# A chain of attentions on one core: two inputs turned by DMA and VectorE, the mask and its row minimum in one operation, the context exponential moved into the copy out of the bank

## The reference

```python
# block 0: two attentions of 16 heads of 16, then a feed-forward
Q = einsum(x, Wq) * m;  K, V = einsum(kv, Wk) * m, einsum(kv, Wv) * m      # m: 0 for a row that is all zero
energy = Q K^T
lengths = sum(energy[:, :, 0, :] != 0, -1)                                # columns past a length are -inf
energy = where(cols > rows, -inf, energy)                                 # self attention alone: causal
score = softmax(energy / sqrt(dk));  out = score V * m
# block 1: layer norm of ctx and of x, an attention of 256 wide, gelu, a second attention on its result
# block 2: softmax(x ctx^T) ctx, added to x
# block 3: an attention of 8 heads of 32 with ctx as keys, a layer norm, then a state that steps through the
#          128 positions: s = silu(s A^T) + u_t
```

## Time and profile before

| what | value |
|---|---|
| median of 3 runs | 4028.19 us (4024.6 to 4034.65) |
| the profiled execution's own time | 4030.49 us |
| its span, first to last instruction | 4028.7 us |
| mean granted TensorE clock | 0.984 |
| busy in the span: PE, DVE, ACT, POOL | 95%, 85%, 87%, 72% |

### The profile page before, as it was taken

How to read it: one execution, slowest core, us unless ns; L and a number is a source line. 1 busy time by engine, 2 the same in 40 slices (tenths; PEclk the granted TensorE clock), 3 DMA queues, 4 the chain that set the end, 5 groups by cost and what they waited for, 6 DMA issues and landing times. The chain is left out here.

```text
span 4028.7 us, 111616 instructions
## 1 busy us (share of the span) xinstructions
PE 3835.5 (95%) x37177; PEld 3207.8 (80%) x37177; DVE 3405.5 (85%) x9519; ACT 3502.7 (87%) x8460; POOL 2895.3 (72%) x3172
## 2 busy tenths in 40 slices
PE   5999999999999999999999999999999999999859
PEld 3788888888888888888888888888888888888637
DVE  3788988888888898888888898888888898888635
ACT  2899999999999999999999999999999999999735
POOL 1577777777777777777777777777777777777635
PEclk7999999999999999999999999999999999999979
DMA  3001011001101100110111011011101100110038
GB/s 114 20 30 34 19 34 34 26 26 34 34 21 32 34 28 24 34 34 21 32 34 31 21 34 34 23 30 35 34 19 34 34 28 24 34 34 24 16 93 303
DMA packets 121875, 159.92 MB, mean 40 GB/s; under 512 B 12296, under 2 KB 108450, under 8 KB 116642
## 3 DMA queue, kind: packets, MB, share of 16 engines
q1 hardware_dynamic: 116896, 145.39, 11.7%
q10 hardware_dynamic: 4416, 7.41, 0.5%
HBM read 114.86 MB, written 37.75 MB: 38 GB/s over the span
## 5 line engine op out<-in xcount | busy, mean ns | idle before, releaser
L621 PE MATMUL bank<-ident,prob 128*128 128x128 f32 x5120 | 757.1, 280 | 62.6 <-ACT CR L1008 24.5
L941 ACT ACTIVATE probT<-bank 128x512 f32<-128x512 f32 x1280 | 733.4, 596 | 93.9 <-PE bank L621 92.5
L621 PEld LDWEIGHTS bank<-ident,prob 128*128 128x128 f32 x5120 | 572.8, 142 | 233.9 <-issue 138.3
L930 ACT ACTIVATE prob<-prob,mx 128x128 f32<-128x128 f32 x2048 | 646.5, 399 | 23.2 <-DVE mx L1130 23.0
L912 ACT ACTIVATE turned<-bank 128x512 f32<-128x512 f32 x896 | 524.5, 603 | 141.0 <-PE bank L557 109.1
L565 PE MATMUL bank<-turned,shared 128*128 128x256 f32 x2560 | 598.8, 381 | 0.7 <-ACT turned L912 0.7
L1447 POOL TENSOR_TENSOR rs_ln<-ve_ln,half 128x2 f32<-128x2 f32 x320 | 251.2, 785 | 444.8 <-DVE ve_ln L1112 444.8
L1141 DVE TENSOR_REDUCE mx<-bank 128x4 f32<-128x512 f32 x768 | 508.9, 684 | 40.7 <-PE bank L592 38.1
L565 PEld LDWEIGHTS bank<-turned,shared 128*128 128x128 f32 x2560 | 474.0, 191 | 59.0 <-ACT turned L912 1.1
L1152 DVE TENSOR_TENSOR prob<-bank,mx 128x512 f32<-128x512 f32 x768 | 509.5, 677 | 6.7
L922 ACT ACTIVATE prob<-prob 128x512 f32<-128x512 f32 x768 | 461.2, 641 | 10.0 <-DVE prob L1152 9.1
(11 more groups left out here) (238 smaller groups left out, 9058.9 us busy)
## 6 DMA issues: line engine op xcount, KB each, us to landing
shared<-in_x SPq DMA_DIRECT2D x128, 256.0 KB, 2.8
CB<-in_ctx SPq DMA_DIRECT2D x64, 256.0 KB, 4.0
CC<-in_ctx SPq DMA_DIRECT2D x64, 256.0 KB, 2.7
mod<-mod_rows SPq DMA_DIRECT2D x64, 256.0 KB, 3.7
residual<-X SPq DMA_DIRECT2D x64, 256.0 KB, 2.2
out<-turned SPq DMA_DIRECT2D x16, 1024.0 KB, 5.0
turned<-residual SPq DMA_DIRECT2D x14, 1024.0 KB, 7.8
u_turned<-us SPq DMA_DIRECT2D x124, 32.0 KB, 1.9
```

The costliest lines, as they stand in the source:

```text
L621: last = nc.tensor.transpose(t[:, h * 128:(h + 1) * 128], src[:, h, :], ident[:])
L930: last = nc.scalar.activation(t[:, h, :], t[:, h, :], ACT.Exp, bias=low[:, h:h + 1], scale=1.0)
L941: nc.scalar.activation(flat(t), banks.of(f"{att}.turn.{b}{r}")[:, :], ACT.Copy).then_inc(*st["act"].mark(f"probT.{b}{r}"))
```

## The change

What it does, part by part:

1. **Inputs turned on the way in.** `x` and `ctx` are loaded by four DMAs each, in runs of 32 elements (128 bytes), so that a 32x32 block transpose on DVE (`nc.vector.transpose`, steps `self_in.xT` and `ctx_in.cT`) gives the turned tile. PE's turns of `xT`, `cT`, `CT` and `ccT` are gone, and with them four copies by ACT. `ccT` is kept for three groups and serves the context attention, block 1, block 2 and block 3.
2. **The row mask of ctx** becomes a DVE multiplication of the turned tile (`masked`), by a row that PE makes with two transposes (`kept`); POOL's `ctx_in.mask` is gone.
3. **The normalised ctx** is made turned, on POOL, by two 128x512 operations (`hcs`, `HCT`) with a scale and a shift row. These rows go out to memory as 4-byte pieces and come back broadcast to 128 partitions (`rowout`, `rowin` on SP). `pair.lnC`, `CT` and the copy of `HCT` are gone from ACT and PE; `NXT` reads SBUF in place of a bank.
4. **Mask and maximum of self attention** become `tensor_tensor_reduce`, four of 128x128 a tile: sum with the mask, sign turned, and its row minimum. Each compiles to two instructions.
5. **Context attention**: PE turns the centred scores, and ACT's copy out of the bank takes the exponential; the eight `exp` steps a group are gone.
6. **Small ones**: values go from the bank straight into `vp`; `count`, `spread`, three `nm` steps, two small copies, `x1r` and POOL's mask copies are gone (rings of two and four buffers in their place).
7. **Order and banks** of all steps are new. `mix_att.scores` and the load of `mod` move from lag 6 to lag 5; the last groups' early load for the scan (`scan_early`) now also waits for `real.av` of the last group, since the new tiles lie where the scan's input goes.

```diff
+                def in_blocks(t, src, g, here):
+                    v = t[:].rearrange("p b d -> p (b d)").rearrange("p (a b k i) -> p a b k i", a=DH, b=G, i=32)
+                    for j in range(4):
+                        sp.dma_start(v[32 * j:32 * j + 32], src[g, j]).then_inc(here.sem, 16)
...
+                    for k, t in enumerate((rs["lnC"], nmr["lnC"])):
+                        sp.dma_start(norm_d[k].rearrange("(b s o) -> s b o", b=G, o=1), t[:].unsqueeze(2), allow_slow_non_contiguous=True)\
+                            .then_inc(norm_out.sem, 16)
...
+                    sp.dma_start(norm_row, norm_d.partition_broadcast(128)).then_inc(norm_in.sem, 16)
...
+                    maker, made = {"self": ("act", "exp"), "ctx": ("dve", "centre"), "mix": ("pool", "part")}[p]
...
+                        for w in latest(free, u_att[maker].done(f"{made}.{b}{r}", g)):
...
+                        last = nc.tensor.transpose(t[:, b * S:(b + 1) * S], keep1[g % 4][:, b:b + 1].to_broadcast([128, 128]), ident[:])
+                    last.then_inc(*ctx_in["pe"].mark("kept"))
...
-                        nc.scalar.activation(flat(t), banks.of(f"{att}.turn.{b}{r}")[:, :], ACT.Copy).then_inc(*st["act"].mark(f"probT.{b}{r}"))
+                        nc.scalar.activation(flat(t), banks.of(f"{att}.turn.{b}{r}")[:, :], ACT.Exp if p == "ctx" else ACT.Copy,
+                                             scale=SCALE[p] if p == "ctx" else 1.0).then_inc(*st["act"].mark(f"probT.{b}{r}"))
...
-                        nc.vector.tensor_tensor(t[:], banks.of(f"{att}.tile.{b}{r}")[:, :].rearrange("p (h t) -> p h t", h=4),
-                                                causal[:].unsqueeze(1).to_broadcast([128, 4, 128]), ALU.add).then_inc(*st["dve"].mark(f"mask.{b}{r}"))
...
-                        nc.vector.tensor_reduce(m[:], probs.of(f"{att}.mask.{b}{r}")[:], AX, ALU.max, negate=True)\
-                            .then_inc(*st["dve"].mark(f"max.{b}{r}"))
...
+                        for h in range(4):
+                            last = nc.vector.tensor_tensor_reduce(t[:, h, :], banks.of(f"{att}.tile.{b}{r}")[:, h * 128:(h + 1) * 128], causal[:],
+                                                                  -1.0, 3.0e38, ALU.add, ALU.min, m[:, h:h + 1])
...
+                    nc.vector.transpose(flat(trn["XT"]), x_blocks.rearrange("p b d -> p (b d)")).then_inc(*self_in["dve"].mark("xT"))
...
+                    nc.vector.transpose(flat(ccT[g % 3]), flat(nat["CB"])).then_inc(*ctx_in["dve"].mark("cT"))
...
+                    nc.vector.tensor_tensor(trn["CBT"][:], ccT[g % 3], t[:, 0:W].unsqueeze(1).to_broadcast([128, DH, W]), ALU.mult)\
+                        .then_inc(*ctx_in["dve"].mark("masked"))
...
+                    nc.gpsimd.tensor_tensor(trn["HCT"][:], ccT[g % 3], norm_row[:, 0, :].unsqueeze(1).to_broadcast([128, DH, W]), ALU.mult)\
+                        .then_inc(*pair["pool"].mark("hcs"))
...
+                    nc.gpsimd.tensor_tensor(trn["HCT"][:], trn["HCT"][:], norm_row[:, 1, :].unsqueeze(1).to_broadcast([128, DH, W]), ALU.add)\
+                        .then_inc(*pair["pool"].mark("HCT"))
...
-                    for w in latest(self_in["pe"].done("xT", n), self_in["dve"].done("amax", n), self_in["pool"].done("keys", n),
+                    for w in latest(self_in["dve"].done("xT", n), self_in["dve"].done("amax", n), self_in["pool"].done("keys", n),
+                                    self_in["pe"].done("v", n), ctx_in["dve"].done("masked", n), pair["pool"].done("HCT", n),
+                                    real["pe"].done("screal", n), real["pe"].done("av", n),
```

More of the change, by code:

```diff
@@ L146 @@
[L146 to L155, removed]
@@ new lines @@
+        ctx_att.back.0@4 ctx_att.back.1@4 ctx_in.q@3 pair.ncT@5 self_att.scores.01@2 self_att.scores.03@2
+        self_att.scores.00@2 mix_att.turn.03@6 pair.sc2@5 ctx_in.k@3 pair.pT2@5 self_att.scores.11@2
+        self_att.scores.02@2 self_att.scores.10@2 mix_att.turn.00@6 pair.av@5 mix_att.turn.01@6
+        self_att.turn.01@2 ffn.x2T@4 mix_att.values.03@6 ctx_in.e0@3 mix_att.values.02@6 mix_att.values.01@6
+        mix_att.values.00@6 self_att.turn.00@2 ffn.fc1@4 self_in.v@2 real.x4T@5 ffn.fc2@4 self_att.turn.03@2
@@ new lines @@
+    mix_in.k:2 ctx_att.out.1:3 ctx_in.x1T:4 ctx_att.back.0:1 mix_att.turn.02:2 ctx_att.back.1:3
+    self_att.tile.00:2 self_att.tile.02:5 self_att.tile.01:3 pair.ncT:0 ctx_in.q:4 pair.sc2:7 mix_att.turn.03:1
+    ctx_in.kept:7 ctx_in.k:4 pair.pT2:1 mix_att.turn.00:3 self_att.tile.10:7 self_att.tile.11:0
+    self_att.tile.03:6 pair.av:1 mix_att.turn.01:2 self_att.turn.01:4 ffn.x2T:6 mix_att.out.0:1 ctx_in.e0:2
+    ffn.fc1:3 self_att.turn.02:2 self_att.turn.00:5 real.x4T:2 ffn.fc2:1 self_in.len:1 self_in.v:6 real.screal:5
@@ L226 @@
+    mix_in.q:4 ctx_att.turn.02:5 ctx_att.turn.03:3 pair.pT1:2 self_in.e0:4 mix_out.u:7 pair.av1:2
 """.split())
@@ L787, in av_wide @@
                     return go
-                def CT(g):
-                    t, free = banks.claim("pair.CT", pair["dve"], "NXT")
-                    for w in latest(free, pair["act"].done("lnC", g)):
-                        pe.wait_ge(*w)
-                    turn4(t, nat["HC"]).then_inc(*pair["pe"].mark("CT"))
                 def u(g):
@@ L1031, in attention @@
                     tiles = [(b, r) for b in BATCHES[p] for r in range(4)]
[L1032 removed]
+                    return {**{f"exp.{b}{r}": exp(p, b, r) for b, r in tiles if p != "ctx"}, **{f"probT.{b}{r}": turn(p, b, r) for b, r in tiles}}
                 def in_order(*names):
@@ L1225, in nz_, with valid_ @@
                             .then_inc(*st["dve"].mark("nz"))
-                    def count(g):
-                        for w in latest(st["dve"].before("spread", g), st["dve"].done("nz", g)):
+                    def valid_(g):
+                        for w in latest(steps[att]["pe"].before("values.", g), st["pe"].done("len", g)):
                             dve.wait_ge(*w)
-                        nc.vector.tensor_reduce(counts[p][:], nz[p][:], AX, ALU.add).then_inc(*st["dve"].mark("count"))
```

424 lines of the change are left out of this document (202 added, 222 removed).

## The result

The changed kernel takes 4046.6 us (median of 8 runs, 4037.6 to 4053.0), the kernel before 4030.6 beside it: a ratio of 1.0038 with a 95% interval from 1.0030 to 1.0047. That is 0.4% slower, where 3922 us and a gain of 2.6% were forecast. 4046.6 lies inside the range of 3865 to 4055, but on the side of "slower", which had a chance of 0.20.

The account below looks back on a forecast made before the run. PE was taken to bound the kernel. From the profiled 4030.5 us, - 97 (PE) - 34 (ACT) + 19 (handoffs) + 6 (end) gave 3924.5, forecast as 3922 us, 2.6% faster, range 3865 to 4055.

Parts of the forecast that it names:

- All of it is covered ... Price 0.: DMA loads of x and ctx in 128-byte pieces and the 4-byte packets: all hidden behind other work, 0 us.
- The rival on small packets: 128-byte load packets taking over some 195 ns make cT wait; 4252 us at 30 us a load, chance 0.03.
- It is hidden by 18 us: At the end, the scan's early load waits for real.av but lands before the scan starts; +6 us, between 0 and +20.
- PE's term: Four turns fewer and two transposes more on PE: 55.9 us needed a group instead of 57.4, -97 us in total.
- ACT's term: Less ACT work halves PE's 68.7 us of waiting for ACT: -34 us.
- The new handoffs: New PE waiting at places such as vp waiting for PE's v: 0.3 us a group, +19 us, between 0 and 60.
- The pairs on DVE: Each of 32 mask-and-minimum instruction pairs a group costs p = 0.27 us, giving DVE 51.0 us, 90% of the new period.
- both rivals on DVE: Short DVE operations take full length, p = 0.45, 3994 us, chance 0.12; or DVE becomes the bound, 4137 us, chance 0.12.
- With p = 0.15 it is 47.2 and nothing more is gained: At 0.15 us a mask pair, DVE needs 47.2 us a group, with no further gain in time.
- New waits eat the gain: The new step order raises PE's idle time from 1.1 to over 2.6 us a group; 4066 us at 3.2, chance 0.05.
- PE's idle time vanishes: PE never waits, so the period is 55.9 us: -168 us, 3862 us, chance 0.04.
- PE at 97 to 98% busy in the steady part: Sign that the forecast is right, along with ACT near 79% and DVE near 90% busy.

Follow-up runs that it names:

- e5: Changed kernel, mean and deviation of ctx turned by an added DVE transpose, stored as 16 pieces of 128 bytes instead of 512 of 4: 3940.2 us.
- e4: Kernel before, plus two stores of 256 4-byte constants to a scratch row ahead of each load of CB, read by nothing: 4178.3 us.
- e8: Kernel before, plus the same 512 4-byte stores a group, each 512 bytes from the next: 4031.0 us, ratio 1.0000 to the kernel before.
- e9: Kernel before, plus 512 4-byte loads a group from ctx into a scratch tile, in place of stores: 4029.6 us, ratio 1.0000.
- e3: Changed kernel, with x and ctx loaded in pieces of 1 KB instead of 128 bytes, 4-byte stores kept: 4075.3 us.
- e1: Changed kernel, with SP issuing the scan's early loads behind the store of u of group 61 instead of ahead: 4059.9 us.
- e7: e5 plus a split early scan load: most no longer waits for real.av, 28 of 122 batches go with the late loads: 3892.9 us.
- e10: Kernel before, with only the context attention change: centred tile turned first, exponential in the copy out of the bank: 4002.7 us, ratio 0.9936.
- e13: e7 with the self attention's old separate mask and maximum put back on DVE: 3950.0 us, ratio 0.9807 to the kernel before.
- e2: Changed kernel, with the 512 4-byte rowout pieces a group replaced by two 1 KB pieces of constants: 3941.4 us, ratio 0.9782 to the kernel before.

## Why the prediction was wrong

Two steps failed, both of them about transfers, and both priced at nothing or next to it.

- **"All of it is covered ... Price 0."** The sum counted the 512 packets of 4 bytes as 1.7 us of DMA time. It measured 106 us: 3642.1 of the changed kernel against 3535.6 of e5, from `x4` to `x4`. Their own busy time is indeed small (544 packets of the queue took 29.5% of 16 engines in the microsecond from 3367, 9 ns each); what they cost is what stands behind them. e4, e8 and e9 show that it is their lying side by side in memory, and the late signals show how it reaches the engines. What makes the signals late stays open. The rival on small packets looked at the 128-byte loads, asked only whether the data comes in time, and had 0.03; e3 clears those loads.
- **"It is hidden by 18 us; SP's later steps queue behind the wait, so between 0 and +20; I take +6."** It measured 47.6 us. The range looked at what waits for the load. The load's own occupation of the queue, 36 us in which a store could not be issued, was not in it. e1 shows that another place in SP's row mends 17 us of it, e7 that all of it goes when most of the load also no longer waits for `real.av`.

That 4046.6 still lies inside the range of 3865 to 4055 is luck: its upper part was made for slow pairs on DVE, which didn't come.

The steps on the engines held, and e7 is where they can be read, since it has the changed kernel's work without the two losses. From `x4` to `x4` it gains 137 us where - 97 - 34 + 19, so 112, were forecast, and its 3892.9 us are 29 below the forecast: without the two losses the sum would have been too cautious.

- **PE's term, 55.9 us a group.** PE's busy share of e7 gives 0.992 x 56.40 = 55.9, against 57.4: 94 us where 97 were taken.
- **ACT's term, half of 68.7 us.** e10: 26.7. In e7 PE idles 0.45 us a group in place of 1.1, 42 us in 64 groups. The new handoffs, taken at +19, cost nothing that can be seen.
- **The pairs on DVE, p = 0.27.** They start 0.21 us apart, and the reading of the accumulator starts with the next pair's first instruction (DVE's timeline of the changed kernel):

```profile
2013.77 0.29 DVE L1131 CUSTOM_DVE_ANT_0 prob<-bank,causal 128x128 f32<-128x128 f32 x1
2013.99 0.08 DVE L1131 DVE_READ_ACCUMULATOR2_ANT mx<- 128x1 f32 x1
2013.99 0.29 DVE L1131 CUSTOM_DVE_ANT_0 prob<-bank,causal 128x128 f32<-128x128 f32 x1
```

  So DVE has 49.2 us a group where 51.0 were expected, and both rivals on DVE fall. The Trainium skill's rule ("VectorE: DVE Perf Modes", "The DRAIN you can't avoid"), which carried the first of them, doesn't hold for these pairs: 0.21 us from start to start, with a length of 0.29 and 0.08. The same section goes on to say that a next operation that is not held starts earlier, which the prediction left out.
- **"With p = 0.15 it is 47.2 and nothing more is gained"**: e13 speaks against this way of thinking, as far as its placing allows. Between 49.2 and 52.2 us of DVE work lie 57 us, though neither is full.
- **The rivals.** None foretold what came. "New waits eat the gain", with 0.05, is the nearest, at 4066: PE's idle time did pass its mark of 2.6 us, but only in the long groups, from late signals and not from the order that it was meant for. Over the steady part PE is idle for 24.55 of 1000 us, some 1.4 us of 58.2, and the 63 periods are still 32 us shorter than before; what turned the gain into a loss is the end, for which there was no rival. (The 3862 of "PE's idle time vanishes" should be 3860, 168 below the 4028 of the others.)

One sign was chosen badly: "PE at 97 to 98% busy in the steady part" came true, at 97.5%, with a period of 58.2 us. At the lower clock PE is busy for longer with the same work, so busy time alone doesn't tell a good period from a bad one.

The sum as measured, in the profiled executions: 4028.7 - 136.4 (to e7) + 47 (the end) + 106 (the stores) = 4045, beside 4044.9. It closes by construction, since the terms are differences of the same profiles.

## What to carry to other kernels

A transfer isn't free because its data comes in time: ask what it holds up, the stores behind it in the same queue and, as here, even the signals between engines. Don't store a column across partitions as single words into neighbouring places; turn it first and store rows. Where a wait has no releaser, ask whether the work that it needs had long been done. And where periods begin to scatter with no wait that explains them, compare a short and a long one microsecond by microsecond before touching the order.

## What the runs showed of the hardware

- 512 stores of 4 bytes a group into the same 2 KB cost the kernel before 150 us (4178.3 against 4028.1 beside it, 2.3 us a group); with 512 bytes between them, or as loads, nothing (4031.0 and 4029.6 against 4030.1 beside them).
- While such stores are under way, signals between engines come late: 3.1 us behind the end of PE's step in the stop at 1632, and over 0.3 us, or with no record, for 519 of 14669 steps, all within 5.1 to 10.5 us of the stores' issue. In e2, e5, e7, e8 and e9, which have no such stores or have them apart, no signal is over 0.3 us late.
- The stop of PE in the long group above cost twice. After the 3.6 us of 3374.7 to 3378.3 the clock granted falls from 1.00 to 0.50, which is 1.2 in place of 2.4 GHz, and is back at 1.00 in 3382 to 3383; four transposes take 1.11 us in that stretch and 0.60 ahead of it. In that group PE is 2 us longer busy than in the short one, with the same matmuls.
- A load of 3904 KB and two of `residual` fill SP's queue so far that the next store's issue takes 36 us.
